# Conditional residual stack on one core: both grouped convs on unrounded fp32 in sixteen 32x32 tiles

## What is computed

```python
x = x + conv(x, W0, groups=4, 9 taps, pad 4) + (cond @ cw0.T + side)[:, :, None]
x = x + einsum('boi,bih->boh', sum_k att1[b, k] * e0[k], x) + bias1(b)[:, :, None]
x = x + einsum('boi,bih->boh', sum_k att2[b, k] * e1[k], x) + bias2(b)[:, :, None]
x = x + conv(x, W3, groups=4, 9 taps, pad 4) + (cond @ cw3.T + side)[:, :, None]
```

## Time and profile before

| | |
|---|---|
| runs | 2600.25, 2599.28, 2600.23 us; median 2600.23 us |
| profiled execution | 2600.42 us; its span on the core 2598.5 us, granted clock 0.995 |
| PE | busy 2554.9 us, 98% |
| DVE, ACT | 88%, 80% |
| DMA | 808.75 MB, mean 311 GB/s |

### The profile page before, as it was taken

The page is one execution under the profiler, slowest core; times in us unless marked ns, Lnnn a source line. Parts: engine busy times, 40 slices in busy tenths (PEclk is TensorE's granted clock), DMA queues, the critical chain, the costliest instruction groups (busy, mean ns, idle before and its releaser), DMA issues.

```text
span 2598.5 us, 38320 instructions
## 1 busy us (share of the span) xinstructions
PE 2554.9 (98%) x11082; PEld 2071.6 (80%) x11082; DVE 2277.4 (88%) x3384; ACT 2077.8 (80%) x1940; POOL 3.7 (0%) x17
## 2 busy tenths in 40 slices
PE   6999999999999999999999999999999999999997
PEld 4788888888888888888888888888888888888885
DVE  7988888888888888888888888888888888888884
ACT  4788878888887888888788888878888887888885
POOL 0000000000000000000000000000000000000000
PEclk8999999999999999999999999999999999999998
DMA  5788888888888888888888888888888888888875
GB/s 193 284 317 317 320 318 314 321 324 316 317 320 318 313 321 324 316 316 320 318 314 321 324 316 316 321 318 313 321 323 317 317 320 317 315 320 322 317 300 210
DMA packets 335448, 808.75 MB, mean 311 GB/s; under 512 B 37066, under 2 KB 40146, under 8 KB 302674
## 3 DMA queue, kind: packets, MB, share of 16 engines
q1 hardware_dynamic: 333200, 807.16, 83.5%
q10 hardware_dynamic: 2242, 1.53, 0.2%
HBM read 137.45 MB, written 134.22 MB: 105 GB/s over the span
## 4 chain that ended last, share of the span: by engine, by line
PE 97%; DVE 2%; issue 0%; DMA 0%; ACT 0%; ACTq 0%; SPq 0%; DVEq 0%
PE pair L766 82%; PE quad L810 14%; PE pair L800 1%; DVE mixed L595 0%; PE quad L747 0%; DMA x_in<-in_x 0%; DVE w_hi L528 0%; DVE weighted L583 0%; DVE x_lo L504 0%; DVE x_lo L630 0%; DVE x_hi L627 0%; DMA x_ph<-x_ch 0%; DVE x_ch L569 0%; DVE w_lo L534 0%; DMA x_ch<-x_ph 0%
## 5 line engine op out<-in xcount | busy, mean ns | idle before, releaser
L766 PE MATMUL pair<-x_hi,w_hi 128*128 128x512 f32 x3072 | 1227.1, 399 | 8.7 <-DVE x_lo L643 5.4
L766 PE MATMUL pair<-x_hi,w_lo 128*128 128x512 f32 x3072 | 1213.1, 395 | 0.0
L766 PE MATMUL pair<-x_lo,w_hi 128*128 128x512 f32 x3072 | 1209.0, 394 | 0.0
L766 PEld LDWEIGHTS pair<-x_hi,w_lo 128*128 128x128 f32 x3072 | 579.6, 189 | 137.3
L766 PEld LDWEIGHTS pair<-x_hi,w_hi 128*128 128x128 f32 x3072 | 579.0, 188 | 136.4 <-DVE x_lo L643 5.8
L766 PEld LDWEIGHTS pair<-x_lo,w_hi 128*128 128x128 f32 x3072 | 581.6, 189 | 131.5
L595 DVE TENSOR_REDUCE mixed<-weighted 128x128 f32<-128x1152 f32 x256 | 576.9, 2254 | 0.1
L402 ACT COPY x_out<-x_ch 128x1024 f32<-128x1024 f32 x256 | 530.3, 2073 | 2.9 <-DMA x_ch<-x_ph 2.9
L351 ACT COPY x_ch<-x_in 128x1024 f32<-128x1024 f32 x256 | 531.0, 2076 | 1.9 <-DMA x_in<-in_x 1.9
L410 ACT COPY x_ph<-pair 128x512 f32<-128x512 f32 x512 | 314.8, 615 | 272.1 <-PE pair L766 272.1
L418 ACT ACTIVATE x_ph<-pair,bias_now 128x512 f32<-128x512 f32 x512 | 358.6, 700 | 216.2 <-PE pair L766 216.2
(11 more groups left out here) (80 smaller groups left out, 607.2 us busy)
## 6 DMA issues: line engine op xcount, KB each, us to landing
x_ph<-x_ch SPq DMA_DIRECT2D x1024, 256.0 KB, 2.6
x_ch<-x_ph SPq DMA_DIRECT2D x1024, 256.0 KB, 2.6
x_in<-in_x SPq DMA_DIRECT2D x128, 1024.0 KB, 5.5
out<-x_out SPq DMA_DIRECT2D x128, 1024.0 KB, 4.2
x_out<-in_W SPq DMA_DIRECT2D x8, 144.0 KB, 5.4
expert<-in_e ACTq DMA_DIRECT2D x2, 512.0 KB, 8.0
x_ph<-in_e_t SPq DMA_DIRECT2D x1, 512.0 KB, 4.3
x_ph<-in_small ACTq DMA_DIRECT2D x1, 458.5 KB, 3.5
```

The lines of the kernel that those rows point to most:

```text
L766: mm = nc.tensor.matmul(conv_bank[g % 2], w[l][:, m, g, :], x[:, g, m:m + N], start=(m == 0 and x is hi and w is w_hi), stop=(m == BLK - 1 ...
```

## The change

Both convs now take x and x3 in plain fp32, unsplit, in the natural layout (channels on the rows). The array is used as sixteen 32x32 tiles: tile (g, p) holds tap t of group g, and streams the segment p (512 positions out of 2048) shifted by t. So channels of group g come from rows 32g to 32g + 31, and the output of segment p goes to rows 32p to 32p + 31 of PSUM bank g. A matmul moves 256 columns: 9 taps x 16 tiles for the first halves of the segments (`FIRST`), then 9 x 16 for the second halves (`REST`), 288 matmuls a conv. No phase moves, cuts, joins or splits of x and x3 are left.

x1 then lies with segments on the rows: output channels of segment p on rows 32p onwards, bank g. The 1x1 product works on that: it has rows of 32 (K=32), four row tiles q at a time, for each group g and each of the three high and low terms, 48 matmuls of 512 columns. Each row tile needs M's rows of group g on its own 32 partitions, so the split M (`m_pair`) is stored to DRAM (`save_m`) and read back to the four row quarters (`spread_m`).

DVE mixes M with 16 multiply-adds of 128x128 a sample, for the sample after next. PSUM is two halves of 4 banks (`banks`), each for one sample at a time: conv 1 of b, then M's product of b in the same half; conv 4 of b - 1 in the other. ACT rounds x1 to x1_hi out of PSUM, DVE subtracts; ACT and DVE share the evacuation of x4. Around it the prologue is rewritten with the same parts (attention, biases, expert vectors).

The core of the diff: PE's part first, then SP's and DVE's new functions.

```diff
+            def conv_taps(l, row, tile, which):
+                for n, t in which:
+                    for p in range(PH):
+                        for g in range(G):
+                            first = N * p + n + t
+                            mm = nc.tensor.matmul(tile[rows_of(p), g, n:n + N // 2],
+                                                  taps[l][rows_of(g), t, g, :],
+                                                  row[rows_of(g), first:first + N // 2],
+                                                  start=(t == 0), stop=(t == TAPS - 1))
+                return mm
+
+            def middle_matrix(b, tile):
+                pe.wait_ge(mix_ready[0], K * (b + 1))
+                pe.wait_ge(mix_ready[1], K * (b + 1))
+                nc.tensor.matmul(tile[:, PH - 1, 0:C], mixed[0][:, :], mixed[1][:, :], start=True,
+                                 stop=True).then_inc(m_done, 1)
+
+            def middle(b, slot, tile):
+                pe.wait_ge(m_spread, DMA * G * (b + 1))
+                pe.wait_ge(x1_split, 2 * b + 2)
+                for g in range(G):
+                    for part, x in ((0, x1_hi), (0, x1_lo), (1, x1_hi)):
+                        for q in range(PH):
+                            mm = nc.tensor.matmul(tile[:, q, :], m_rows[rows_of(q), slot, g, part, :],
+                                                  x[rows_of(q), g, :],
+                                                  start=(g == 0 and part == 0 and x is x1_hi),
+                                                  stop=(g == G - 1 and part == 1))
+                mm.then_inc(mid_done, 1)
+
+            BOTH = [(n, t) for n in (0, N // 2) for t in range(TAPS)]
+            FIRST = BOTH[0:TAPS]
+            REST = BOTH[TAPS:]
+
+            def step(b, slot, turn, last=False):
+                loaded, evacuated = DMA * (turn + 1), 2 * (b - 1)
+                if not isinstance(b, int):
+                    loaded, evacuated = pe.to_reg(loaded), pe.to_reg(evacuated)
+                pe.wait_ge(taps_ready, 1)
+                pe.wait_ge(x_loaded[slot], loaded)
+                wait(pe, x4_ready, evacuated)
+                conv_taps(0, x_in[:, slot, :], banks[slot], FIRST)
+                pe.wait_ge(x3_ready, 2 * b)
+                if not last:
+                    middle_matrix(b + 1, banks[1 - slot])
+                conv_taps(0, x_in[:, slot, :], banks[slot], REST).then_inc(conv1_done, 1)
+                pe.wait_ge(taps_ready, 2)
+                if not last:
+                    pe.wait_ge(m_ready, b + 2)
+                conv_taps(1, x3, banks[1 - slot], BOTH).then_inc(conv4_done, 1)
+                middle(b, slot, banks[slot])
...
-            def conv(l, g, hi, lo, done):
-                for m in range(BLK):
-                    for w, x in ((w_hi, hi), (w_hi, lo), (w_lo, hi)):
-                        mm = nc.tensor.matmul(conv_bank[g % 2], w[l][:, m, g, :], x[:, g, m:m + N],
-                                              start=(m == 0 and x is hi and w is w_hi),
-                                              stop=(m == BLK - 1 and w is w_lo))
-                mm.then_inc(done, 1)
...
-            def middle(b):
-
-                wait(pe, x3_ready, 2 * b)
-                pe.wait_ge(m_split, 2 * b + 2)
-                for q in range(PH):
-                    pe.wait_ge(x1_split, PH * b + q + 1)
-                    for m, x in ((m_hi, x1_hi), (m_hi, x1_lo), (m_lo, x1_hi)):
-                        mm = nc.tensor.matmul(mid_bank[:, q, :], m[:, :], x[:, q, :],
-                                              start=(m is m_hi and x is x1_hi), stop=(m is m_lo))
-                    mm.then_inc(mid_done, 1)
-
-            def step(b):
-                middle_matrix(b)
-                conv1(b)
-                conv4(b - 1)
-                middle(b)
...
+            def save_m(b, slot):
+                sp.wait_ge(m_split, b + 1)
+                sp.dma_start(m_saved[slot, :, :, :], m_pair[:, :, :].bitcast(f32)).then_inc(m_stored, DMA)
+
+            def spread_m(b, slot):
+                sp.wait_ge(m_stored, DMA * (b + 1))
+                for q in range(PH):
+                    sp.dma_start(m_rows[rows_of(q), slot, :, :, :].bitcast(f32),
+                                 m_saved[slot, :, :, :].rearrange("(g c) t o -> c g t o", g=G)
+                                 ).then_inc(m_spread, DMA)
+
+            def store(b, slot):
+                sp.wait_ge(x4_ready, 2 * b + 2)
+                rows = out[b, :, :].rearrange("(g o) (p n) -> p o g n", g=G, p=PH)
+                for p in range(PH):
+                    sp.dma_start(rows[p], x4[rows_of(p), slot, :, :]).then_inc(x_stored[slot], DMA)
...
+            def high_x1(b, tile):
+                act.wait_ge(conv1_done, b + 1)
+                for half in range(2):
+                    nc.scalar.copy(halves(x1_hi, half), halves(tile, half)).then_inc(x1_high, 1)
+
...
+            def mix_experts(b):
+                for k in range(K):
+                    for l in range(2):
+                        if k == 0:
+                            wait(dve, m_done, b)
+                        else:
+                            dve.wait_ge(mix_ready[l], K * b + k)
+                        nc.vector.scalar_tensor_tensor(mixed[l][:, :], expert[l][:, k, :],
+                                                       mix[l][:, b, k:k + 1],
+                                                       ident[:, :] if k == 0 else mixed[l][:, :],
+                                                       ALU.mult, ALU.add).then_inc(mix_ready[l], 1)
```

More of the change, by code:

```diff
@@ L229, in wait, with halves @@
                 eng.wait_ge(s, value)
+        def halves(tile, half):
+            return tile[:, half * PH // 2:(half + 1) * PH // 2, :]
         block = ctx.enter_context(nc.Block())
@@ L303, in _ @@
-            move_x(0)
-            sp.dma_start(expert_t, a["e0_t"].rearrange("k r c -> r k c")).then_inc(expert_t_loaded, DMA)
-            load(1, 1)
-            place_taps(1)
-            load(2, 0)
-            for b in range(2):
-                step(b, b, whole=False)
-            with sp.Fori(1, (B - 4) // 2) as i:
-                for odd in range(ODD):
-                    step(2 * i + odd, odd)
-            for b in range(B - 4, B):
-                step(b, b % ODD, whole=False)
-            move_x3(B - 1)
@@ L323, in _ @@
+            save_m(0, 0)
+            spread_m(0, 0)
+            for b in range(ODD):
+                step(b, b, early=b)
+            with sp.Fori(1, B // ODD - 1) as i:
+                for odd in range(ODD):
+                    step(ODD * i + odd, odd)
+            for b in range(B - ODD, B):
+                step(b, b % ODD, load_next=False, last=(b == B - 1))
+            for b in range(B - ODD, B):
+                store(b, b % ODD)
             for slot in range(ODD):
-                sp.wait_ge(x_stored[slot], DMA * B // ODD)
+                sp.wait_ge(x_stored[slot], DMA * PH * B // ODD)
@@ new lines, in evacuate_x4, with evacuate_x3 @@
+            def evacuate_x4(b, slot, turn, tile):
+                wait(act, x_stored[slot], DMA * PH * turn)
+                act.wait_ge(bias4_ready, b + 1)
+                act.wait_ge(conv4_done, b + 1)
+                for g in range(G // 2):
+                    done = nc.scalar.activation(x4[:, slot, g, :], tile[:, g, :], ACT.Identity,
+                                                bias=bias4_now[:, slot, g:g + 1])
+                done.then_inc(x4_ready, 1)
+            def evacuate_x3(b, slot, tile):
+                act.wait_ge(bias3_ready, b + 1)
+                act.wait_ge(mid_done, b + 1)
+                for half in range(2):
+                    columns = x3[:, EDGE:L + EDGE].rearrange("c (p n) -> c p n", p=PH)
+                    nc.scalar.activation(halves(columns, half), halves(tile, half), ACT.Identity,
+                                         bias=bias3_now[:, slot:slot + 1]).then_inc(x3_ready, 1)
@@ L431, in step @@
-            def step(b, slot, turn, first=False, last=False):
-                evacuate_x1(b, 0)
-                if not first:
-                    join(b - 2, slot, turn - 1, 0)
-                evacuate_x1(b, 1)
-                if not first:
-                    join(b - 2, slot, turn - 1, 1)
-                evacuate_x1(b, 2)
-                evacuate_x1(b, 3)
-                for g in range(G):
-                    if not (isinstance(b, int) and b == 0):
-                        evacuate_x4(b - 1, g)
-                    if g == 0 and not (last and slot == 1):
-                        round_x(b + 1)
-                    if not last and g in (1, 2):
-                        cut(b + 2, slot, turn + 1, g - 1)
-                evacuate_x3(b)
@@ L690, in _ @@
[L690 to L704 removed]
+            dve.wait_ge(experts_loaded, 2 * DMA)
@@ L707, in _ @@
+            with dve.Fori(2, B // ODD - 1) as i:
+                for odd in range(ODD):
+                    step(ODD * i + odd, odd, i)
```

(5 more changed lines are left out.)

654 lines of the change are left out of this document (210 added, 444 removed).

## The result

The changed kernel takes 5227.3 us (median of 4 runs, 5212.94 to 5249.22) against 2599.93 us: ratio 2.011, 95% interval 2.004 to 2.018. The prediction was 2650 us, range 2480 to 5100. The profiled execution has a span of 5210.2 us, 2612 us more than before.

The account below looks back on a forecast made before the run. PE was taken as the bound, busy 98%. A sample: convs 16.1, product 2.8, middle matrix 0.22, shape changes 0.65, loop turn 0.35, so 20.1 us against 19.75; +45 us gives 2645, set at 2650 us, range 2480 to 5100.

Parts of the forecast that it names:

- Can PE's sequencer feed them?: Issue of 2304 PE instructions a sample: 12.9 us at 5.6 ns each, hidden behind the convs' 16.1 us.
- The turn of the loop: PE's loop branch, with a possible code fetch: 0.7 us a turn, 0.35 us a sample (0 to 1.3 us).
- The bound of 11 ns: Upper reading of PE's time per instruction from the earlier trace; 2304 instructions would take 25 us.
- If 16 tiles stream at a time ... 72 packs of passes: 16.1 us: Convs: 1152 passes a sample run 16 at once, 16.1 us (15.4 to 16.7) against 16.7 before.
- Rival 2: Conv packs don't close up, as tiles drain between passes: 26 to 32 us a sample, 3400 to 4170 us; chance 0.17.
- Small terms: Beside the convs, a sample: product 2.8 us, middle matrix 0.22, shape changes 0.65; DVE 9.8 and ACT 5.9 us hidden.
- m's trip: m's way through DRAM on SP's queue: down at about 14 us, needed 24 us later, so free.
- a way to be wrong: Sign of error: PE's granted clock falls to the 1.2 GHz level in the steady part.
- Rival 3: PE's weight loads come one after another: 39 us a sample, 5050 us; chance 0.13.
- Feeding at 11 ns: Part of Rival 2: PE's instructions issue at 11 ns each, 25 + 3.8 us a sample.

Follow-up runs that it names:

- e13: e2 with 128 columns in each matmul instead of 256 (half the positions get two taps, the others one): 1927.38 us.
- e9: The changed kernel with taps 0 to 2 alone, run three times in an inner loop, so its number of matmuls comes from a third of the code: 3759.42 us.
- e7: e4 with the matmuls reordered, three taps of one tile in a row before the next tile: 10572.32 us.
- e4: The changed kernel with 512 columns in each conv matmul and taps 0 to 5 alone: 2159.97 us.
- e2: The changed kernel with taps 0 to 2 alone in both convs, 256 columns: 1803.38 us.
- e1: The changed kernel with conv matmuls of 512 columns instead of two of 256, all 9 taps: 3314.69 us, ratio 1.273.
- e10: e9 with 512 columns in each conv matmul (taps 0 to 2, run three times in an inner loop): 2972.0 us.

## Why the prediction was wrong, step by step

**The step that failed** is "Can PE's sequencer feed them?", with its tail "The turn of the loop". It took 5.6 ns an instruction from the earlier trace rows, and as a price of issue that was not too low: 64 instructions ran in 0.41 us in e13, and inside a pack a load and a matmul start every 7 ns. But it is the price of code that is already there; before's loop was 180 instructions. The text gave the turn one fetch, at most 1.3 us a sample, and took the rest of the new body as resident. In truth all of it comes in again each turn, at some 4 us for 256 instructions, 16 ns each: 2404 instructions a sample are 9.4 packets, 10 in the trace, and these make the 40.2 us. The bound of 11 ns was a bound on issue, not on fetching. Against e9 it costs 11.5 us a sample, and e9 itself still has a gap of 2.9 us a turn, 1.5 us a sample.

**"If 16 tiles stream at a time ... 72 packs of passes: 16.1 us".** The condition was right for the start of a pack (16 starts in 0.1 us), and the pass is 0.213 us, the lower end. But a pack of 16 two-pass tiles takes 0.2 us more: 36 packs of 0.63 to 0.64 us are 22.8 us. Rival 2 priced this at 5.8 us with 0.17 chance; it measured 7.4. So its price was near by luck: the mechanism named there, a tile that drains, is wrong, since packs of 8 have no surplus.

**Small terms.** The product was 3.0 us for 2.8, the middle matrix with its shape changes 0.4 for 0.87. The resident sum is 22.8 + 3.0 + 0.4 = 26.2 us, e9's undisturbed sample 26.5. DVE has 1142.0 / 128 = 8.9 us for 9.8, ACT 5.4 for 5.9, and PE waits for neither, nor for m's trip. The granted clock did fall, which I had named as a way to be wrong: 0.939 in the mean, behind gaps, as a consequence of supply.

**The whole**, a sample: 19.75 before; -1.3 for conv streaming (15.4 for 16.7); +7.4 for packs that don't close up; +0.4 for product and changes; +2.6 for the loop's turn and its clock (e9's 28.8 less 26.2); +11.4 for the rest of supply: 40.2.

**Range and rivals.** The measured 5227 us lies above the whole range. Rival 3's 5050 us was near it by luck, for a reason that the first trace refutes. "Feeding at 11 ns" and "the turn" held the right question at a fraction of its price.

**What stays open:** what the rule of the surplus is (none at 8 and 12 tiles, 0.2 us at 16, none for single bf16 passes, e7 far worse). A short look-ahead of PE may have to do with it, but no run measures one. In e4's packs the passes start some 17 ns apart, with stops of about 0.2 us in between, and what holds them is not shown. Why a packet takes about 4 us wasn't tried either: 1.7% of 16 engines over 5210.2 us is 1.1 us of transfer for each of the 1276, so most of it is something else, and whether the kernel's other DMAs delay it is untested. Nor is it known why e9's body is fetched and e2's is not. No version here beats before: e1, 3315 us, is the best full one, and e10 bounds a resident one at 2972. Only packs without surplus (18 x 0.853 + 3.4 = 18.8 us a sample, about 2470 us) would, and no order found gives them.

## What to carry to other kernels

Count the instructions of an engine's loop body before splitting its matmuls into tiles: past the size that stays (here between 1740 and 2260 on PE, and with inner loops already at some 1740) the body is fetched each turn, and each 256 instructions need some 4 us of work to hide behind. The instruction queue's packets in the page show it at once: tens, or hundreds. A price per instruction read from a short loop says nothing of a long one. And unrounded fp32 in 16 tiles is two passes to a tile at half the column rate plus 0.2 us a pack; use the widest columns that PSUM takes.

## What the runs showed that was not expected

- Matmuls start out of program order across tiles (conv 4's first before conv 1's last passes), but only over a short distance: six passes in a row on a tile leave 13 tiles idle (10572 us for 2160).
- Less work can take longer: with half the columns e13 has 1924.8 us of span for e2's 1800.8, since PE is at the 1.2 GHz level behind 72 of its 128 longer waits (mean clock 0.897).
- Code that is there takes 64 PE instructions in 0.41 us; fetched code 256 in about 4 us.
- A loop with inner loops was fetched anew each turn (570 packets) at a length that stays without them (20 packets).
